# Splitting the second halves of short products around the score matmuls, and taking the projection before the first maxima

## The chip, the cores and the metric

The kernel runs on one core of a Trainium2 chip. The metric is device time in microseconds (us) of one execution, from launch to the last output in memory. TensorE (PE in the rows; PEld is its weight load), VectorE (DVE), ScalarE (ACT), GpSimd (POOL) and SyncE (SP, which issues the transfers) each run their own instruction stream and meet through semaphores.

## The reference

One transformer block on x of shape (8, 512, 256), fp32: a layer norm, then multi-head attention and a gated feed-forward layer side by side, and a residual.

```python
xn  = layernorm(x)                               # over the 256 channels
qkv = xn @ qkv_w + qkv_b                         # 16 heads of 16 channels
att = softmax(q @ k.T / 4) @ v                   # per head, 512 x 512 scores
out = x + (att @ proj_w + proj_b) \
        + (silu(xn @ (w_gate/127).T) * (xn @ (w_up/127).T)) @ (w_down/127).T
```

The feed-forward hidden size is 768; its weights are integers from -127 to 127.

## The kernel before, in words

**Precision by parts.** An fp32 operand is kept as a high and a low fp32r part, and a product is a sum of terms high x high, low x high and high x low. A weight that is exact in its high part needs two terms instead of three; the feed-forward weights are, and the kernel finds that out at run time and takes the shorter branch.

**Rows and steps.** "Row" is one of the 8 batch entries. The work of a row is cut into 16 steps of a software pipeline (`STEPS`), in which a step s works on four heads (group s // 4) and 128 keys (s % 4). In each step TensorE does, in this order (`step`, L1326 on):

1. `scores_t(s, 0)`: the transposed scores of two heads, two matmuls into `st_bank` (L1077). It waits until ScalarE has taken the previous content (`exp_done`).
2. the second half of the step's product (`end_product`, L1264)
3. `scores(.., 0)`: scores for six steps later, two matmuls into `s_bank` (L1094), needed for the row maxima alone. It waits until VectorE has reduced the previous content (`max_done`).
4. `probs_v`: probabilities times values of the step before, eight matmuls into `o_bank` in the trace (L1110)
5. in four of the steps a small transpose of maxima (L1208)
6. `scores_t(s, 1)`, then `scores(.., 1)`, as 1 and 3, for the other two heads
7. the first half of the next step's product (`begin_product`, L1254)

For long products (down, and q1 with k1) item 2 comes after item 3 instead.

ScalarE takes the exponential of each transposed score bank (L743), one instruction per item 1 or 6, and VectorE takes the maxima of each score bank (L889), again two per step. There is one `st_bank` and one `s_bank`, so each score matmul waits for the reader of the last one.

**Products in halves.** A product is made with matmuls of 64 rows of contraction, two at a time in the upper and lower half of the array, each writing its own PSUM bank. The first half pass (`half_product(spec, 0)`) sends rows 0 to 63 to bank A and 64 to 127 to bank B; the second (`swap=1`) exchanges them. As both passes add to the same banks, the second starts with a wait for `half_made`, which the last matmul of the first increments. A "term" below is one such pair of matmuls.

**The table.** `STEADY` (L65) says in which step each product ("chunk") stands: up4 with gate4 in step 0, v1 in 1, up5 in 2, the transposes of xn in 3, proj0 (of the row before) in 4, q0 in 5, k0 in 6, proj1 in 7, q1 with k1 in 8, down0 and down1 in 9 and 10, up0 to up3 with their gates in 11 to 14, v0 in 15. A half pass has 6 terms of 2 x 256 columns for v, q0, k0 and proj; 4 terms of 2 x 512 columns for up with gate. The last entry of a chunk is its PSUM banks of `dense`, three in all: proj0 uses (0, 1) and q0 behind it (1, 2); proj1 uses (0, 1), and q1 with k1 behind it 2 and 0.

**Who takes a product.** ScalarE takes v, q, k and up in slot 0 of their step, after the exponential of item 1; the gate goes to ScalarE and VectorE after item 6. proj and down are added to `resid` by VectorE (L919), in slot 0 after the maxima of item 3: in `step` of VectorE `maxima(row, s, slot // 2)` comes first, and then `take(row, chunk)` for `("proj", "down")`.

## Time and profile before

| | |
|---|---|
| median of 3 runs | 610.33 us (609.66 to 615.7) |
| profiled execution, its own time | 611.8 us |
| its span | 610.0 us |
| TensorE busy | 579.2 us (95%), 5012 matmuls |
| VectorE busy | 427.1 us (70%) |
| ScalarE busy | 421.2 us (69%) |
| GpSimd busy | 300.1 us (49%) |
| mean granted TensorE clock | 0.991 of full speed |
| chain that ended last | TensorE 82%, ScalarE 6%, VectorE 5% |

The page of the profile gives these sums; the rest is read from the timeline, which lists instructions by start time and merges equal ones that follow each other. A matmul's printed duration is longer than the distance to the next one, since they are pipelined, so what a block of matmuls costs on TensorE is the distance from its start to the start of the next block. A row of the timeline that starts later than the one before it would allow has its idle time in brackets only if no matmul is still in flight.

### The profile page before, as it was taken

The page shows a single profiled execution, that of the slowest core. Times are in us where ns is not written, and L with a number is a line of the kernel's source. Part 1 is how long each engine was busy: PE and PEld are TensorE (multiplying, and loading weights), DVE is VectorE, ACT ScalarE, POOL GpSimd, SP SyncE. Part 2 cuts the span into 40 slices and gives each one's busy share as a digit, 9 for nine tenths or more (in the row PEclk, how much of TensorE's full clock was granted, in tenths as well). Part 3 has the DMA queues.
Part 4 walks back from the last instruction along what each step waited for, and adds up shares of the span by engine and source line. Part 5 has one row for each costly group of instructions (what it writes and reads, how often), then busy time and mean ns, then how long its engine had stood idle before and what let it go on. Part 6 is the DMA issues. An engine that isn't in the chain of part 4 may idle for free.

```text
span 610.0 us, 14095 instructions
## 1 busy us (share of the span) xinstructions
PE 579.2 (95%) x5012; PEld 344.2 (56%) x5012; DVE 427.1 (70%) x514; ACT 421.2 (69%) x604; POOL 300.1 (49%) x303
## 2 busy tenths in 40 slices
PE   7888799999999999999999999999999999998896
PEld 6655356555755557555665567555665557553533
DVE  5886667777777767777777776777677866777722
ACT  3556675887577866878667866787658875776562
POOL 3234737644475526754465535844376444354210
PEclk9999999999999999999999999999999999999989
DMA  8790146122822147222742128221661118220101
GB/s 263 240 153 2 37 139 172 32 52 81 230 84 54 53 134 161 53 52 76 190 133 53 35 108 204 52 53 53 183 157 31 29 70 233 66 54 19 54 2 37
DMA packets 38609, 59.20 MB, mean 97 GB/s; under 512 B 6320, under 2 KB 21680, under 8 KB 38576
## 3 DMA queue, kind: packets, MB, share of 16 engines
q1 hardware_dynamic: 38576, 58.75, 36.0%
q8 instruction: 22, 0.36, 0.3%
q14 instruction: 11, 0.09, 0.1%
HBM read 37.23 MB, written 20.97 MB: 95 GB/s over the span
## 4 chain that ended last, share of the span: by engine, by line
PE 82%; ACT 6%; DVE 5%; issue 3%; DMA 1%; POOL 1%; SPq 0%; DVEq 0%; POOLq 0%
PE dense L1136 33%; PE o_bank L1110 19%; PE st_bank L1077 14%; PE s_bank L1094 10%; ACT probs L743 3%; PE dense L1120 2%; DVE resid L919 1%; DVE neg_max L889 1%; PE dense L1200 1%; DMA probs<-in_L_attn_qkv_w 1%; PE dense L1208 1%; POOL xn L637 1%; ACT max_whole L784 1%; ACT probs L821 1%; PE dense L1189 0%
## 5 line engine op out<-in xcount | busy, mean ns | idle before, releaser
L889 DVE TENSOR_REDUCE neg_max<-s_bank 128x2 f32<-128x1024 f32 x250 | 306.0, 1224 | 135.7 <-PE s_bank L1094 135.7
L743 ACT ACTIVATE probs<-st_bank 128x1024 f32<-128x1024 f32 x250 | 256.8, 1027 | 120.0 <-PE st_bank L1077 117.3
L1110 PE MATMUL o_bank<-probs,v_ones 128*32 128x512 f32 x1024 | 138.1, 612 | 0.0
L1077 PE MATMUL st_bank<-q_stack,k_stack 50*128 50x512 f32 x500 | 121.1, 480 | 8.3 <-ACT probs L743 7.0
L1077 PEld LDWEIGHTS st_bank<-q_stack,k_stack 50*128 50x128 f32 x500 | 47.4, 184 | 115.0 <-ACT probs L743 72.8
L1094 PE MATMUL s_bank<-k_stack,q_stack 48*128 48x512 f32 x500 | 109.1, 431 | 1.9 <-DVE neg_max L889 1.8
L652 POOL TENSOR_TENSOR hid_tl<-gated,hid_th 128x512 fp32r<-128x512 f32 x48 | 61.7, 1286 | 35.1 <-ACT hid_th L835 35.1
L646 POOL TENSOR_TENSOR gated<-gated,hid 128x512 f32<-128x512 f32 x48 | 61.7, 1285 | 34.6 <-DVE gated L911 18.5
L1094 PEld LDWEIGHTS s_bank<-k_stack,q_stack 48*128 48x128 f32 x500 | 47.3, 184 | 25.5 <-DVE neg_max L889 20.1
L1136 PE MATMUL dense<-xn_th,w_uh 64*128 64x512 f32 x176 | 57.0, 403 | 1.2 <-ACT v_ones L775 0.8
L1136 PE MATMUL dense<-xn_th,w_gh 64*128 64x512 f32 x176 | 57.3, 405 | 0.0
L1136 PE MATMUL dense<-xn_tl,w_gh 64*128 64x512 f32 x176 | 54.9, 391 | 0.0
L1136 PE MATMUL dense<-xn_tl,w_uh 64*128 64x512 f32 x176 | 54.9, 391 | 0.0
L664 POOL TENSOR_TENSOR qk_parts<-raw_d,qk_parts 128x512 fp32r<-128x512 f32 x28 | 35.8, 1289 | 27.8 <-ACT qk_parts L812 27.8
L679 POOL TENSOR_TENSOR o_norm<-o_blocks,inv_sum 128x256 f32<-128x256 f32 x31 | 19.3, 623 | 59.0 <-DVE inv_sum L934 58.7
L705 POOL TENSOR_TENSOR resid<-resid,p_bias 128x256 f32<-128x256 f32 x32 | 22.9, 737 | 48.3 <-DMA resid<-in_L_attn_x 48.3
L1110 PEld LDWEIGHTS o_bank<-probs,v_ones 128*32 128x32 f32 x1024 | 20.2, 108 | 37.1 <-issue 26.8
L637 POOL TENSOR_SCALAR xn<-xn,moments,rstd 128x256 f32<-128x256 f32 x28 | 33.9, 1224 | 1.3 <-POOL rstd L631 1.3
L911 DVE SCALAR_TENSOR_TENSOR gated<-gated,dense 128x512 f32<-128x512 f32 x48 | 32.2, 670 | 3.4 <-ACT gated L789 2.1
L1136 PEld LDWEIGHTS dense<-xn_tl,w_gh 64*128 64x128 f32 x176 | 32.4, 184 | 3.7
L1136 PEld LDWEIGHTS dense<-xn_tl,w_uh 64*128 64x128 f32 x176 | 32.4, 184 | 3.3
L930 DVE STREAM_TRANSPOSE o_blocks<-o_bank 128x512 f32<-128x512 f32 x31 | 22.0, 709 | 16.1 <-PE o_bank L1110 16.1
(147 smaller groups left out, 855.9 us busy)
## 6 DMA issues: line engine op xcount, KB each, us to landing
q_spread<-qk_parts SPq DMA_DIRECT2D x16, 512.0 KB, 3.5
k_spread<-qk_parts SPq DMA_DIRECT2D x16, 512.0 KB, 3.7
q_stack<-q_spread SPq DMA_DIRECT2D x64, 128.0 KB, 3.1
k_stack<-k_spread SPq DMA_DIRECT2D x64, 128.0 KB, 3.3
q_stack<-q_spread SPq DMA_DIRECT2D x64, 64.0 KB, 3.3
k_stack<-k_spread SPq DMA_DIRECT2D x64, 64.0 KB, 3.3
resid<-in_L_attn_x SPq DMA_DIRECT2D x16, 256.0 KB, 3.6
out<-resid SPq DMA_DIRECT2D x15, 256.0 KB, 2.2
```

The source lines that it names most:

```text
L637: nc.gpsimd.tensor_scalar(xn[:, t, :], xn[:, t, :], moments[:, t, 0:1], rstd[:, t:t + 1], ALU.subtract, ALU.mult).then_inc(xn_done, 1)
L646: nc.gpsimd.tensor_tensor(gated[:, m % 2, :], gated[:, m % 2, :], hid[:, m % 2, :], ALU.mult).then_inc(hid_product, 1)
L652: nc.gpsimd.tensor_tensor(hid_t[1][:, m, :], gated[:, m % 2, :], hid_t[0][:, m, :].bitcast(F32), ALU.subtract).then_inc(hid_low, 1)
L664: nc.gpsimd.tensor_tensor(low, whole[:, WHOLE_AT[kind, i], :], high.bitcast(F32), ALU.subtract).then_inc(split_low, 1)
L705: nc.gpsimd.tensor_tensor(resid[:, t, :], resid[:, t, :], p_bias[:, :], ALU.add).then_inc(resid_ready, 1)
L743: nc.scalar.activation(probs[:, s % 2, 2 * half:2 * half + 2, :], transposed_bank(row, s, half)[:, :, :], ACT.Exp, scale=SCALE).then_inc(e ...
L889: nc.vector.tensor_reduce(neg_max[:, g % 2, :, NT * pair + qt], score_bank(row, half)[:, :, :], AX_X, ALU.max, negate=True).then_inc(max_d ...
L911: nc.vector.scalar_tensor_tensor(part, part, 1.0, bank, ALU.add, ALU.mult).then_inc(dve_free, 1)
L1077: done = nc.tensor.matmul(transposed_bank(row, s, half)[:, r, :], k_stack[rows, pair, P * kt:P * (kt + 1)], q_stack[rows, pair, :], start= ...
L1094: done = nc.tensor.matmul(score_bank(row, half)[:, r, :], q_stack[rows, pair, P * qt:P * (qt + 1)], k_stack[rows, pair, :], start=True, st ...
L1110: done = nc.tensor.matmul(o_bank[32 * j:32 * (j + 1), :], v_ones[:, kt, 8 * (g // 2) + 2 * j + g % 2, :], probs[:, (s - 1) % 2, j, :], sta ...
L1136: done = nc.tensor.matmul(banks[h], stationary(h, a, k)[rows], moving(h, b, k)[rows], start=swap == 0 and n == 0, stop=swap == 1 and n == ...
```

## The change

A table `ENDS` gives for each short kind of product how many terms of the second half pass stand ahead of `scores_t(s, 0)` and how many behind `scores(.., 0)`; what is left stays between them. (4, 2) for v, q, k: four terms, the transposed scores, the scores, two terms. (6, 0) for proj: all six terms, the transposed scores, the scores. (0, 1) for up: the transposed scores, three terms, the scores, one term. Long products stay as they were. The wait for `half_made` stands before the first term of the pass, wherever that is. On VectorE the take of proj moves ahead of the maxima of its slot; the take of down stays behind.

```diff
--- before.py
+++ after.py
@@ -80,6 +80,9 @@
     (14, 0, "up", 3, 1, (1,)), (14, 0, "gate", 3, 1, (0,)), (14, 1, "max", 0, 1, (2,)),
     (15, 0, "v", 0, 1, (1, 2)),
 ]
+
+
+ENDS = {"v": (4, 2), "q": (4, 2), "k": (4, 2), "proj": (6, 0), "up": (0, 1)}
 
 TOGETHER = {("up", i): ("gate", i) for i in range(KH)} | {("q", 1): ("k", 1)}
 WPREP = ("wgate", "wup", "wdown")
@@ -1027,10 +1030,13 @@
                         averaged = averaged_at(row, s, slot)
                         if averaged is not None:
                             statistics_done(averaged)
+                        for chunk in chunks_at(row, s, slot):
+                            if chunk[2] == "proj":
+                                take(row, chunk)
                         if slot in (0, 2) and pair_ahead(row, s, slot // 2):
                             maxima(row, s, slot // 2)
                         for chunk in chunks_at(row, s, slot):
-                            if chunk[2] in ("proj", "down"):
+                            if chunk[2] == "down":
                                 take(row, chunk)
                         if measured and measured[0] == 0:
                             dve.wait_ge(x_in, 16 * measured[1])
@@ -1121,13 +1127,16 @@
                                                 stop=n == len(parts) - 1 and k == tiles - 1)
                 return done
 
-            def half_product(spec, swap):
+            def terms_in(spec):
+                return sum(len(those) for _, those in spec[3])
+
+            def half_product(spec, swap, some=slice(None)):
 
 
 
                 banks, stationary, moving, stages = spec
                 terms = [(ready if n == 0 else None, term) for ready, those in stages for n, term in enumerate(those)]
-                for n, (ready, (a, b, k)) in enumerate(terms):
+                for n, (ready, (a, b, k)) in list(enumerate(terms))[some]:
                     if ready is not None and swap == 0:
                         pe.wait_ge(*ready)
                     for r in range(2):
@@ -1261,10 +1270,20 @@
                     pe.wait_ge(ot_low1, row.at)
                 half_product(spec_of(row, chunk, exact), 0).then_inc(half_made, 1)
 
-            def end_product(row, chunk, exact):
-
-                pe.wait_ge(half_made, products_up_to(row, chunk))
-                half_product(spec_of(row, chunk, exact), 1).then_inc(dense_done, len(made_together(row, chunk)))
+            def end_product(row, chunk, exact, part):
+
+
+                spec = spec_of(row, chunk, exact)
+                of_all = terms_in(spec)
+                ahead, behind = (0, of_all) if long_product(chunk) else ENDS[chunk[2]]
+                some = (slice(0, ahead), slice(ahead, of_all - behind), slice(of_all - behind, of_all))[part]
+                if some.start == some.stop:
+                    return
+                if some.start == 0:
+                    pe.wait_ge(half_made, products_up_to(row, chunk))
+                done = half_product(spec, 1, some)
+                if some.stop == of_all:
+                    done.then_inc(dense_done, len(made_together(row, chunk)))
 
             def project_first_half():
 
@@ -1329,14 +1348,16 @@
                     here = product_at(row, s)
                     if here and s == 0:
                         begin_product(row, here, exact)
+                    if here:
+                        end_product(row, here, exact, 0)
                     if row.has(0):
                         scores_t(row, s, 0)
-                    if here and not long_product(here):
-                        end_product(row, here, exact)
+                    if here:
+                        end_product(row, here, exact, 1)
                     if pair_ahead(row, s, 0):
                         scores(row, s, 0)
-                    if here and long_product(here):
-                        end_product(row, here, exact)
+                    if here:
+                        end_product(row, here, exact, 2)
                     if after_scores(row, s):
                         scores_t(row, s, 1)
                     if row.like == ROWS and s == 0:
```

In the three pairs of fences below a name such as `dense<-xn_th,w_gh` is the bank written and the operands read; L1136 before and L1145 now is the matmul of `half_product`, L1077 and L1083 the transposed scores (`st_bank`), L1094 and L1100 the scores (`s_bank`), L1110 and L1116 the probabilities times values (`o_bank`).

TensorE, a q product (also v and k), from the first half pass to `probs_v`, before:

```order
L1136 MATMUL dense<-w_qkvh,xn_th 128x256 x4
L1136 MATMUL dense<-w_qkvh,xn_tl 128x256 x4
L1136 MATMUL dense<-w_qkvl,xn_th 128x256 x4
L1077 MATMUL st_bank<-q_stack,k_stack 128x512 x2
L1136 MATMUL dense<-w_qkvh,xn_th 128x256 x4
L1136 MATMUL dense<-w_qkvh,xn_tl 128x256 x4
L1136 MATMUL dense<-w_qkvl,xn_th 128x256 x4
L1094 MATMUL s_bank<-k_stack,q_stack 128x512 x2
L1110 MATMUL o_bank<-probs,v_ones 32x512 x4
```

and now:

```order
L1145 MATMUL dense<-w_qkvh,xn_th 128x256 x4
L1145 MATMUL dense<-w_qkvh,xn_tl 128x256 x4
L1145 MATMUL dense<-w_qkvl,xn_th 128x256 x4
L1145 MATMUL dense<-w_qkvh,xn_th 128x256 x4
L1145 MATMUL dense<-w_qkvh,xn_tl 128x256 x4
L1083 MATMUL st_bank<-q_stack,k_stack 128x512 x2
L1100 MATMUL s_bank<-k_stack,q_stack 128x512 x2
L1145 MATMUL dense<-w_qkvl,xn_th 128x256 x4
L1116 MATMUL o_bank<-probs,v_ones 32x512 x4
```

Nothing stands between the two half passes any more; the transposed scores have moved back by four terms, and two terms have moved behind the scores.

TensorE, the second half pass of an up product with its gate, before:

```order
L1077 MATMUL st_bank<-q_stack,k_stack 128x512 x2
L1136 MATMUL dense<-xn_th,w_gh 128x512
L1136 MATMUL dense<-xn_th,w_uh 128x512
L1136 MATMUL dense<-xn_th,w_gh 128x512
L1136 MATMUL dense<-xn_th,w_uh 128x512
L1136 MATMUL dense<-xn_tl,w_gh 128x512
L1136 MATMUL dense<-xn_tl,w_uh 128x512
L1136 MATMUL dense<-xn_tl,w_gh 128x512
L1136 MATMUL dense<-xn_tl,w_uh 128x512
L1094 MATMUL s_bank<-k_stack,q_stack 128x512 x2
```

and now:

```order
L1083 MATMUL st_bank<-q_stack,k_stack 128x512 x2
L1145 MATMUL dense<-xn_th,w_gh 128x512
L1145 MATMUL dense<-xn_th,w_uh 128x512
L1145 MATMUL dense<-xn_th,w_gh 128x512
L1145 MATMUL dense<-xn_th,w_uh 128x512
L1145 MATMUL dense<-xn_tl,w_gh 128x512
L1145 MATMUL dense<-xn_tl,w_uh 128x512
L1100 MATMUL s_bank<-k_stack,q_stack 128x512 x2
L1145 MATMUL dense<-xn_tl,w_gh 128x512
L1145 MATMUL dense<-xn_tl,w_uh 128x512
```

The scores have moved one term forward.

VectorE around the take of proj0 (`resid<-dense,resid`), before:

```order
L889 TENSOR_REDUCE neg_max<-s_bank 128x2
L898 ISA
L917 ISA
L919 TENSOR_TENSOR resid<-dense,resid 128x512
L926 REGISTER_ALU
L929 REGISTER_ALU
L930 STREAM_TRANSPOSE o_blocks<-o_bank 128x512
L888 REGISTER_ALU
L889 TENSOR_REDUCE neg_max<-s_bank 128x2
```

and now:

```order
L901 ISA
L920 ISA
L922 TENSOR_TENSOR resid<-dense,resid 128x512
L891 ISA
L892 TENSOR_REDUCE neg_max<-s_bank 128x2
L929 REGISTER_ALU
L932 REGISTER_ALU
L933 STREAM_TRANSPOSE o_blocks<-o_bank 128x512
L891 REGISTER_ALU
L892 TENSOR_REDUCE neg_max<-s_bank 128x2
```

The maxima of the step's first scores now stand behind the take, and so behind the end of the whole projection product.

## Rows read from the trace of the kernel before

**Rows 1.** Timeline of TensorE, step 5 into 6 (k0): start us, us, engine, line, instruction.
```profile
283.61 1.06 PE L1110 MATMUL o_bank<-probs,v_ones 128*32 128x512 f32 x8
284.61 0.50 PE L1077 MATMUL st_bank<-q_stack,k_stack 50*128 50x512 f32 x2
285.00 0.50 PE L1094 MATMUL s_bank<-k_stack,q_stack 48*128 48x512 f32 x2
285.35 0.40 PE L1136 MATMUL dense<-xn_th,w_qkvh 64*128 64x256 f32 x4
...
286.22 0.50 PE L1077 MATMUL st_bank<-q_stack,k_stack 50*128 50x512 f32 x2
286.56 0.40 PE L1136 MATMUL dense<-xn_th,w_qkvh 64*128 64x256 f32 x4
...
287.26 0.39 PE L1094 MATMUL s_bank<-k_stack,q_stack 48*128 48x512 f32 x2
287.58 1.07 PE L1110 MATMUL o_bank<-probs,v_ones 128*32 128x512 f32 x8
```

**Rows 2.** Timeline of ScalarE in step 5: the exponential of the second transposed scores.
```profile
285.14 1.03 ACT L743 ACTIVATE probs<-st_bank 128x1024 f32<-128x1024 f32 x1 [0.85 <-PE st_bank L1077]
```

**Rows 3.** Timeline of TensorE, step 13 into 14 (up3), one row earlier.
```profile
251.16 0.51 PE L1077 MATMUL st_bank<-q_stack,k_stack 50*128 50x512 f32 x2
251.55 0.50 PE L1094 MATMUL s_bank<-k_stack,q_stack 48*128 48x512 f32 x2
251.89 0.39 PE L1136 MATMUL dense<-xn_th,w_uh 64*128 64x512 f32 x1
...
252.82 0.46 PE L1077 MATMUL st_bank<-q_stack,k_stack 50*128 50x512 f32 x2
253.12 0.43 PE L1136 MATMUL dense<-xn_th,w_uh 64*128 64x512 f32 x1
...
254.09 0.40 PE L1094 MATMUL s_bank<-k_stack,q_stack 48*128 48x512 f32 x2
```

**Rows 4.** Timeline of VectorE: the maxima just before the scores at 251.55.
```profile
250.27 1.23 DVE L889 TENSOR_REDUCE neg_max<-s_bank 128x2 f32<-128x1024 f32 x1 [0.49 <-PE s_bank L1094]
```

**Rows 5.** Timeline of TensorE over proj0 and the start of q0.
```profile
276.96 0.70 PE L1136 MATMUL dense<-w_ph,ot_parts 64*128 64x256 f32 x8
...
278.92 0.40 PE L1094 MATMUL s_bank<-k_stack,q_stack 48*128 48x512 f32 x2
...
280.66 0.48 PE L1094 MATMUL s_bank<-k_stack,q_stack 48*128 48x512 f32 x2
281.43 0.51 PE L1136 MATMUL dense<-xn_th,w_qkvh 64*128 64x256 f32 x4 [0.29 <-DVE resid L919]
```

**Rows 6.** Timeline of VectorE beside it.
```profile
279.36 1.23 DVE L889 TENSOR_REDUCE neg_max<-s_bank 128x2 f32<-128x1024 f32 x1 [0.97 <-PE s_bank L1094]
280.50 0.68 DVE L919 TENSOR_TENSOR resid<-dense,resid 128x512 f32<-128x512 f32 x1
```

**Rows 7.** Timeline of TensorE: proj1 starts its first half, and q1 behind it.
```profile
289.36 0.64 PE L1136 MATMUL dense<-w_ph,ot_parts 64*128 64x256 f32 x8
...
293.77 0.72 PE L1136 MATMUL dense<-xn_th,w_qkvh 64*128 64x512 f32 x4
```

**Rows 8.** Timeline of TensorE around a wait for half_made (step 5, q0).
```profile
282.01 0.41 PE L1136 MATMUL dense<-xn_tl,w_qkvh 64*128 64x256 f32 x4
...
282.49 0.49 PE L1136 MATMUL dense<-xn_th,w_qkvh 64*128 64x256 f32 x4
282.81 0.40 PE L1136 MATMUL dense<-xn_th,w_qkvl 64*128 64x256 f32 x4
```

**Rows 9.** Timeline of the weight loads (PEld) at the same place.
```profile
282.47 0.30 PEld L1136 LDWEIGHTS dense<-xn_th,w_qkvh 64*128 64x128 f32 x4 [0.15 <-PE dense L1136]
```

**Rows 10.** Timeline of TensorE in step 9, a long product, where no score matmul waits.
```profile
300.22 0.40 PE L1077 MATMUL st_bank<-q_stack,k_stack 50*128 50x512 f32 x2
300.46 0.40 PE L1094 MATMUL s_bank<-k_stack,q_stack 48*128 48x512 f32 x2
```

## The prediction

> **What bounds the kernel now.** The table of busy times comes first: TensorE is busy for 95% of the span and holds 82% of the chain that ended last, ScalarE and VectorE are busy for about 70%. So a step lasts as long as TensorE's stream of blocks, and the question is which distances between blocks are longer than the work in them. That is read from the timeline, start to start.
>
> Take the step around k0 [rows 1]. A pair of score matmuls costs 0.24 us where nothing waits [rows 10]. After `probs_v` (1.00 us, 283.61 to 284.61) the second transposed scores take 0.39 and the second scores 0.35; the first half pass takes 0.87 (285.35 to 286.22), although the second, of the same matmuls, takes 0.70 (286.56 to 287.26); the first transposed scores take 0.34 and the first scores 0.32. The 0.17 us in the first half pass is a stall: the exponential of the bank filled at 284.61 runs from 285.14 to 286.17 [rows 2], and only then, at 286.22, may the bank be written. So **transposed scores must be at least 1.61 us apart**. Each score matmul that really waits costs 0.10 us more than 0.24 as well, since its weight load no longer lies under earlier matmuls. In the same way **scores must be about 1.71 us apart**: 0.44 from their start to VectorE (278.92 to 279.36 in [rows 5, 6]), 1.23 for the maxima, 0.05 back (251.50 to 251.55 in [rows 3, 4]).
>
> The first half pass of an up product is longer (0.93) and meets the 1.61 nearly by itself [rows 3]: the second transposed scores at 251.16, the first at 252.82. There the second scores are late, at 0.39 behind the transposed ones instead of 0.34, and take 0.34 instead of 0.24, because VectorE ends at 251.50 [rows 4].
>
> **The change part by part.** In every sum below a pair of scores is 0.24 without a wait and 0.34 with one or directly behind `probs_v`; the last block ahead of `probs_v` pays 0.09 more (0.32 instead of 0.24 at 287.26 to 287.58 [rows 1]), whichever block that is.
>
> *The wait for half_made.* In v, q, k and proj it now follows directly on the first half pass. How long TensorE then stands is not in the trace, but its parts are. The last pair of the first half starts near 282.13 (the row at 282.01 holds two pairs, 0.12 apart [rows 8]) and its record ends at 282.42. The load that waited for it starts at 282.47 [rows 9], so 0.34 after the last pair started, where the next pair would have started after 0.12: 0.22 lost. The first four matmuls behind that wait take 0.32 to the next block instead of 0.24 [rows 8], so 0.08 to 0.10 more. I take **0.32 us per wait**, with 0.10 (the load alone) and 0.45 as ends, the upper one if the semaphore takes 0.13 longer to come back when the engine is empty. There are six such products in a row of the batch: 1.9 us, which is what the moves must earn back.
>
> What the trace shows of this tail is the end of a record and a semaphore. The Trainium skill (TensorE: Matmul & The Clock Gate, Single matmul latency and Back-to-back issue gap) gives an isolated matmul of 256 columns (398 + 256) / 2.4 = 272 ns against a gap of 109 ns in a stream. By that page alone the exposed tail would be an estimated 0.16 us instead of 0.32, and the sum 6 x 0.16 x 7 = 7 us lower; the rows here show 0.28 for the record, and the semaphore and the load besides.
>
> *v, q and k (4, 2).* The new step is 0.34 (transposed) + 0.24 (scores: the last ones are now 0.24 + 0.32 + 1.00 + 0.34 = 1.90 back, over 1.71) + 0.70 + 0.32 + 0.47 (four terms) + 0.24 + 0.24 (the other bank was filled 2.07 before, over 1.61) + 0.32 (two terms) + 1.00 = 3.87, against 3.97 now (283.61 to 287.58 [rows 1]). The gap to the next transposed scores is 0.24 + 0.24 + 0.32 + 1.00 = 1.80, again over 1.61. That is 0.10; with the unrounded 0.235 for a pair it is 0.12. I take **0.12 for each of k0, v1 and v0: 0.36**. The takes on ScalarE have cover: an exponential (from 0.5 after the matmul, 1.03 long) and a take (by VectorE's of the same size 0.6) end 2.1 after the transposed scores, and the next exponential can start 2.3 after.
>
> *proj (6, 0) and its take.* For proj0 [rows 5, 6]: the first half starts at 276.96 and lasts 0.70, the wait 0.32, the second half 0.70, so the transposed scores stand at 278.68 and the scores at 278.92, which is where they are today. The product is complete at about 278.84, VectorE takes it from 278.88, and 0.60 later (0.68 less the 0.09 by which the next instruction overlaps, as 279.36 + 1.23 = 280.59 is followed at 280.50) starts the maxima: 279.48 instead of 279.36. They end at 280.71; the second scores start at 280.76 instead of 280.66. This is the new wait, 0.10 us. But q0 today starts at 281.43 only, because it writes a bank of proj0 that VectorE empties behind the maxima; now that bank is long free and q0 starts at 280.76 + 0.34 = 281.10: **0.33 gained**. q0 itself pays its 0.32 and loses the penalty of 0.10 twice: its stretch to `probs_v` goes from 2.18 (281.43 to 283.61) to 0.70 + 0.32 + 0.47 + 0.24 + 0.24 + 0.32 = 2.29: 0.11 lost. Together **0.22**.
>
> For proj1 [rows 7]: 289.36 + 0.70 + 0.32 + 0.70 = 291.08 for the transposed scores, take from 291.28, maxima from 291.88 to 293.11, second scores 293.16, and q1 with k1 at 293.50 instead of 293.77: **0.27**.
>
> *up (0, 1).* One term goes behind the scores, so the scores are 0.24 + 0.32 + 1.00 + 0.34 = 1.90 ahead of the next and the wait of [rows 4] goes. What is late next is the exponential: 0.34 + 0.24 + 0.93 = 1.51 is under 1.61, so the transposed scores wait for it. From transposed scores to the next ones past `probs_v`: 1.61 + 0.34 + 0.70 + 0.24 + 0.32 + 1.00 = 4.21, against 2.93 + 0.33 + 1.00 = 4.26 now [rows 3]. **0.05 for each of six: 0.3.** So two thirds of what is moved here is given back at once.
>
> *Long products and the xn step* keep their order: 0. SyncE and GpSimd get nothing new; a proj take that comes sooner lets its store be issued sooner, beside other work.
>
> The sum is 0.36 + 0.22 + 0.27 + 0.3 = 1.15 us per row of the batch. v0, q, k and up0 to up3 occur in rows 0 to 6, proj in rows 1 to 7, v1, up4 and up5 in all eight: seven sets, 8.05 us. From the profiled execution's 611.8 that gives 603.8; the median of the runs was 1.5 below that execution, so **602.3 us**.
>
> **The rivals.**
>
> *A. The predicted chain of small gains, 599 to 605.* For it: every distance used stands in a row, and the step with no waiting scores shows that satisfied waits cost nothing [rows 10].
>
> *B. Nothing measurable, 605 to 610.* The drain costs its upper end, 0.45: 6 x 0.13 x 7 = 5.5 us less gain, leaving 2.5 (607.8). Or ScalarE's takes fall behind in the up steps, where the product is complete 0.24 later. For it: the drain with nothing behind it is the only length not seen whole. Against it: the load at 282.47 started within 0.06 of the record's end.
>
> *C. Slower, 612 to 625.* The weight loads behind the half_made wait and around the split groups are no longer pulled under earlier matmuls: each score pair in the changed place, and each term group behind it, pays 0.10 although its wait is satisfied. That is four more in v and k steps (3.87 + 0.40 = 4.27 against 3.97, three times 0.3), two more in up steps (4.41 against 4.26, six times 0.15), four in q0 and two in each proj (0.8, against the 0.49 of the pairs): 0.9 + 0.9 + 0.3 = 2.1 us per row, 15 us, so 625 at worst. It decides from about 11 such loads per row, where the 1.15 is gone. Against it stands [rows 10]; for it only that satisfied waits straight behind an emptied engine are not in the trace.
>
> *D. More than predicted, 595 to 599.* The drain costs only its lower end, 0.10, because the load may pass earlier than in [rows 9]: 6 x 0.22 x 7 = 9 us more at the most (593). Against it: the second pass cannot start before the first has ended.
>
> **How the numbers follow.** Chances: A 0.55, B 0.24, C 0.09, D 0.12. The likeliest case gives 602.3. The range reaches from 597.5, into D, to 608.5, into B, and leaves out C, the top of B and the bottom of D, about 0.2. What a measurement of this kernel can tell from no change is 1%, 6.1 us: faster means under 604.2, slower over 616.4. A's upper edge lies just past that line, so of A some 0.47 counts as faster, with D 0.59, and 0.01 of B; same is the rest of A and B and a part of C, 0.32; slower 0.08.
>
> **What would show it.** In the profile of the changed kernel: in the k0 step the distance from the end block of the first half pass to the second should be 0.32 longer than the matmuls in them, the transposed scores and the scores there should stand 0.24 apart, and `probs_v` to `probs_v` should be 3.87. q0's first matmul should follow the second scores by 0.34 with no idle time released by `resid`. In up steps scores should follow the second transposed ones at once and the first transposed ones should wait for ScalarE. Wrong would be the sum if score pairs without a wait took 0.34, if the take of proj delayed the second scores by over 0.3, or if the gap in front of the second half pass were over 0.45.

## The result, and the profile after

The changed kernel takes 606.27 us against 611.95 for the one before (medians of 13 runs each); the ratio is 0.9904, 95% interval 0.9878 to 0.993. The ratio leaves out one run of the changed kernel, 611.86, which fell into the chip's slower state. A second set of runs gave 0.992 (0.989 to 0.9951). The prediction was 602.3, from 597.5 to 608.5, and 8 us gained; by the two ratios 5.9 and 4.9 us were.

The profiled execution has a span of 603.0 us, 7.0 less than before. Not all of it is the change: the first half of the first up4, ahead of which no edited instruction stands, starts at 47.74 instead of 49.65. The first `probs_v` starts at 54.17 instead of 56.05, so the two edited steps between gain nothing (6.43 against 6.40). In the traces of this case that second point lies anywhere between 53.7 and 56.3, whatever the kernel. From there to the end 5.1 us are gone.

The chain that ended last, from the page of the changed kernel, by engine:

```profile
PE 84%; DVE 6%; ACT 3%; issue 2%; DMA 1%; POOL 1%; SPq 0%; DVEq 0%; POOLq 0%
```

ScalarE's share has halved, from 6% to 3%: the exponential was what the transposed scores waited for. VectorE's has gone from 5% to 6%.

The best instrument here is the step table. Each entry is the distance in us from one `probs_v` to the next on TensorE, the median of rows 1 to 4 of the batch. An entry is named by the product whose halves lie in it, so it also holds the second transposed scores and second scores of the step before. Such medians agree within some 0.02 between runs of one kernel, while whole runs of one kernel scatter over 1%. The granted clock was 1.00 in these rows in every trace used here.

| | before | changed | difference | predicted |
|---|---|---|---|---|
| k0, v1 | 3.99, 3.99 | 3.88, 3.88 | -0.22 | -0.24 |
| v0 | 4.20 | 4.20 | 0 | -0.12 |
| proj0 + q0 | 4.11 + 4.34 | 4.17 + 4.32 | +0.05 | -0.22 |
| proj1 + q1k1 | 4.20 + 5.45 | 4.09 + 5.30 | -0.26 | -0.27 |
| up0, up1, up2, up3, up5 | 21.49 | 21.37 | -0.12 | -0.25 |
| up4 | 4.61 | 4.35 | -0.26 | -0.05 |
| xn, down0, down1 | 13.63 | 13.65 | +0.02 | 0 |
| row of the batch | 69.99 | 69.20 | -0.80 | -1.15 |

**k0** came as worked out. TensorE in the changed kernel, the stretch that answers to [rows 1]:

```profile
279.42 1.06 PE L1116 MATMUL o_bank<-probs,v_ones 128*32 128x512 f32 x8
280.42 0.50 PE L1083 MATMUL st_bank<-q_stack,k_stack 50*128 50x512 f32 x2
280.76 0.39 PE L1100 MATMUL s_bank<-k_stack,q_stack 48*128 48x512 f32 x2
280.99 0.40 PE L1145 MATMUL dense<-xn_th,w_qkvh 64*128 64x256 f32 x4
...
281.46 0.40 PE L1145 MATMUL dense<-xn_tl,w_qkvh 64*128 64x256 f32 x4
281.92 0.50 PE L1145 MATMUL dense<-xn_th,w_qkvh 64*128 64x256 f32 x4
...
282.49 0.40 PE L1083 MATMUL st_bank<-q_stack,k_stack 50*128 50x512 f32 x2
282.73 0.40 PE L1100 MATMUL s_bank<-k_stack,q_stack 48*128 48x512 f32 x2
282.97 0.40 PE L1145 MATMUL dense<-xn_tl,w_qkvh 64*128 64x256 f32 x4
283.30 0.64 PE L1116 MATMUL o_bank<-probs,v_ones 128*32 128x512 f32 x4
```

Read start to start: transposed scores 0.34, scores 0.23 (0.35 before, when they waited for VectorE), then ten terms and the wait for `half_made` in 1.50 (280.99 to 282.49), which without the wait would be 1.17. So **the wait costs 0.33**; 0.32 was taken. It shows as 281.46 to 281.92, 0.46 where four matmuls take 0.23, and as 0.34 instead of 0.23 for the four behind it. The transposed scores and the scores stand 0.24 apart, neither waiting.

**up** came as worked out in kind. The stretch that answers to [rows 3]:

```profile
247.40 0.51 PE L1083 MATMUL st_bank<-q_stack,k_stack 50*128 50x512 f32 x2
247.74 0.40 PE L1100 MATMUL s_bank<-k_stack,q_stack 48*128 48x512 f32 x2
247.97 0.39 PE L1145 MATMUL dense<-xn_th,w_gh 64*128 64x512 f32 x1
...
249.02 0.50 PE L1083 MATMUL st_bank<-q_stack,k_stack 50*128 50x512 f32 x2
249.36 0.39 PE L1145 MATMUL dense<-xn_th,w_gh 64*128 64x512 f32 x1
```

The second scores follow after 0.34 and take 0.23, where they took 0.34 before. But the first transposed scores stand at 247.40 + 1.62: the exponential's distance, now binding in full. The step takes 4.21, as forecast, but up0 and up1 gain 0.01 and nothing.

**proj0 and q0** did not. TensorE in the changed kernel, the stretch that answers to [rows 5]:

```profile
272.74 0.70 PE L1145 MATMUL dense<-w_ph,ot_parts 64*128 64x256 f32 x8
...
273.73 0.74 PE L1145 MATMUL dense<-w_ph,ot_parts 64*128 64x256 f32 x8
274.30 0.40 PE L1145 MATMUL dense<-w_pl,ot_parts 64*128 64x256 f32 x4
274.54 0.40 PE L1083 MATMUL st_bank<-q_stack,k_stack 50*128 50x512 f32 x2
274.77 0.40 PE L1100 MATMUL s_bank<-k_stack,q_stack 48*128 48x512 f32 x2
...
276.11 0.50 PE L1083 MATMUL st_bank<-q_stack,k_stack 50*128 50x512 f32 x2
276.72 0.49 PE L1100 MATMUL s_bank<-k_stack,q_stack 48*128 48x512 f32 x2
277.06 0.45 PE L1145 MATMUL dense<-xn_th,w_qkvh 64*128 64x256 f32 x4
```

and VectorE beside it, as in [rows 6]:

```profile
274.85 0.69 DVE L922 TENSOR_TENSOR resid<-dense,resid 128x512 f32<-128x512 f32 x1 [0.68 <-PE dense L1145]
275.45 1.22 DVE L892 TENSOR_REDUCE neg_max<-s_bank 128x2 f32<-128x1024 f32 x1
```

The idle time at q0 that `resid` ended is gone, as foretold. From the start of the first half pass to q0 it is now 4.32 instead of 4.47 in [rows 5], though: 0.15 gained and not 0.33. Two places are late. The two passes took 1.80 (272.74 to 274.54), where 1.72 was reckoned and 1.74 is what proj1 takes; no run here shows what the 0.06 more than at proj1 are. And the last matmul's record ends at 274.70, the take starts at 274.85: 0.15 for a step that costs VectorE 0.04 to 0.05 at the scores. It starts the maxima 0.60 later, and they end at 276.67, just before the second scores at 276.72. From the first matmul of the product those scores stand at 3.98, against 3.70 before and 3.80 forecast. q0 itself, from its first matmul to `probs_v`, takes 2.36 (277.06 to 279.42) instead of 2.18, where 2.29 was forecast.

### The profile page after: what moved, and what is told of

It is laid out like the page before. It is cut to its first block, busy times and chain, and to the rows that moved or that the text cites. A ratio compares the mean times of both kernels' runs of the same rounds, so it can differ in the third digit from the quotient of the medians.

```text
span 603.0 us, 14095 instructions
## 1 busy us (share of the span) xinstructions
PE 574.4 (95%) x5012; PEld 346.2 (57%) x5012; DVE 430.5 (71%) x514; ACT 423.4 (70%) x604; POOL 300.2 (50%) x303
## 4 chain that ended last, share of the span: by engine, by line
PE 84%; DVE 6%; ACT 3%; issue 2%; DMA 1%; POOL 1%; SPq 0%; DVEq 0%; POOLq 0%
PE dense L1145 37%; PE o_bank L1116 19%; PE st_bank L1083 14%; PE s_bank L1100 10%; DVE neg_max L892 4%; PE dense L1126 2%; PE dense L1209 1%; PE dense L1217 1%; DMA probs<-in_L_attn_qkv_w 1%; ACT probs L746 1%; POOL xn L640 1%; ACT probs L824 1%; PE dense L1198 0%; DVE w_gl L925 0%; DMA q_stack<-max_tl 0%
## 5 line engine op out<-in xcount | busy, mean ns | idle before, releaser
L1116 PE MATMUL o_bank<-probs,v_ones 128*32 128x512 f32 x1024 | 137.6, 610 | 0.0
L1083 PE MATMUL st_bank<-q_stack,k_stack 50*128 50x512 f32 x500 | 118.9, 471 | 6.3 <-ACT probs L746 5.4
L1083 PEld LDWEIGHTS st_bank<-q_stack,k_stack 50*128 50x128 f32 x500 | 47.3, 184 | 110.7 <-ACT probs L746 67.9
L1100 PE MATMUL s_bank<-k_stack,q_stack 48*128 48x512 f32 x500 | 104.3, 412 | 2.5 <-DVE neg_max L892 1.1
L1145 PE MATMUL dense<-xn_tl,w_gh 64*128 64x512 f32 x176 | 61.8, 391 | 0.0
L1145 PE MATMUL dense<-xn_tl,w_uh 64*128 64x512 f32 x176 | 61.8, 391 | 0.0
L1100 PEld LDWEIGHTS s_bank<-k_stack,q_stack 48*128 48x128 f32 x500 | 47.5, 185 | 17.6 <-DVE neg_max L892 12.6
L1145 PE MATMUL dense<-xn_th,w_uh 64*128 64x512 f32 x176 | 55.8, 396 | 0.8 <-ACT v_ones L778 0.8
L1145 PE MATMUL dense<-xn_th,w_gh 64*128 64x512 f32 x176 | 56.0, 397 | 0.0
L1116 PEld LDWEIGHTS o_bank<-probs,v_ones 128*32 128x32 f32 x1024 | 20.2, 108 | 34.8 <-issue 21.1
L1145 PEld LDWEIGHTS dense<-xn_tl,w_gh 64*128 64x128 f32 x176 | 32.5, 185 | 3.9
L1145 PEld LDWEIGHTS dense<-xn_tl,w_uh 64*128 64x128 f32 x176 | 32.5, 185 | 3.0
```

Source lines behind the costliest of these rows:

```text
L1083: done = nc.tensor.matmul(transposed_bank(row, s, half)[:, r, :], k_stack[rows, pair, P * kt:P * (kt + 1)], q_stack[rows, pair, :], start= ...
L1100: done = nc.tensor.matmul(score_bank(row, half)[:, r, :], q_stack[rows, pair, P * qt:P * (qt + 1)], k_stack[rows, pair, :], start=True, st ...
L1116: done = nc.tensor.matmul(o_bank[32 * j:32 * (j + 1), :], v_ones[:, kt, 8 * (g // 2) + 2 * j + g % 2, :], probs[:, (s - 1) % 2, j, :], sta ...
L1145: done = nc.tensor.matmul(banks[h], stationary(h, a, k)[rows], moving(h, b, k)[rows], start=swap == 0 and n == 0, stop=swap == 1 and n == ...
```

## Experiments

All step figures are the medians of rows 1 to 4, as in the table. The kernels of experiments 1 to 8 ran once each, so their whole times are not compared.

**1. The up products alone.** `ENDS` with (0, 1) for up and (0, 0) for the rest, the take as before.

```diff
-ENDS = {"v": (4, 2), "q": (4, 2), "k": (4, 2), "proj": (6, 0), "up": (0, 1)}
+ENDS = {"v": (0, 0), "q": (0, 0), "k": (0, 0), "proj": (0, 0), "up": (0, 1)}
```

> Only the up products are split, (0, 1); v, q, k, proj and the take as before. Theory 1 (the parts are independent, and each step's gain belongs to its own edit): up steps 12 to 14 and 2 last 4.21 us as in the changed kernel (4.25 before), with the exponential as their new limit; step 0 keeps the changed kernel's 4.35 (4.60 before); k0 stays at 3.99, proj0 with q0 at 8.45, proj1 with q1 at 9.65. A row of the batch then lasts 69.6 us instead of 70.0. Theory 2 (the parts lean on each other): step 0 gains only because v0 ahead of it was changed too, and stays at 4.6; a row 69.85.

Measured: a row 69.91. up2 4.21 and up3 4.23 as expected, but up4 4.60, not 4.35. up1 (4.29) and up5 (4.25) gain nothing either, where 4.21 was expected. So the parts do lean on each other, and the large gain at up4 is not of the up edit. The 0.03 that up5 gains in the changed kernel isn't either: it comes back in experiment 2 (4.22), with v1 split and up not. This kernel and the changed one at the start of up4's step, second transposed scores, second scores and the first matmul of up4; first this kernel:

```profile
260.16 0.50 PE L1080 MATMUL st_bank<-q_stack,k_stack 50*128 50x512 f32 x2
260.56 0.49 PE L1097 MATMUL s_bank<-k_stack,q_stack 48*128 48x512 f32 x2
261.15 0.49 PE L1142 MATMUL dense<-xn_th,w_uh 64*128 64x512 f32 x1
```

then the changed kernel:

```profile
255.80 0.50 PE L1083 MATMUL st_bank<-q_stack,k_stack 50*128 50x512 f32 x2
256.14 0.39 PE L1100 MATMUL s_bank<-k_stack,q_stack 48*128 48x512 f32 x2
256.54 0.49 PE L1145 MATMUL dense<-xn_th,w_uh 64*128 64x512 f32 x1
```

Here the loop over the batch branches back, between the second scores and up4. With v0 unsplit the scores wait for VectorE (0.40 behind the transposed ones), and up4 is 0.59 behind them. With v0's two terms behind the first scores they do not wait (0.34), and up4 follows after 0.40. That the instructions around the branch can be worked off ahead only when the scores do not block the stream fits this, since the 0.19 between 0.59 and 0.40 is more than the 0.10 of an exposed load; in the trace of before, where the written-out rows at the end of the batch have no branch between, up4 follows after 0.34 (469.97 to 470.31) with the scores waiting just the same. No run here shows the branch by itself.

**2. v, q and k alone.**

```diff
-ENDS = {"v": (4, 2), "q": (4, 2), "k": (4, 2), "proj": (6, 0), "up": (0, 1)}
+ENDS = {"v": (4, 2), "q": (4, 2), "k": (4, 2), "proj": (0, 0), "up": (0, 0)}
```

> Only v, q0 and k0 are split, (4, 2); up, proj and the take as before. Theory 1: k0 and v1 last 3.88 (3.99 before), v0 4.20 as before, since its first half waits 0.10 for a bank and that wait used to lie under the exponential's. q0 loses about 0.1 to the drain but still starts late behind the take of proj0: proj0 with q0 8.55 (8.45 before). A row: 70.0 - 0.22 + 0.1 = 69.9. Theory 2 (the drain costs more where the engine is not kept waiting anyway): v0 slower than 4.25 and k0 over 3.92.

Measured: a row 69.85, k0 3.88, v0 4.20. up4 is 4.35, which settles experiment 1: v0's split gives up4 its 0.25. It is the two terms behind the scores and not the four ahead, since up4 keeps its 4.35 in experiment 7, where none stand ahead. v1 is 4.03 and not 3.88: its second scores wait again, as up4's last term no longer stands behind the first ones. And q0 is 4.56, 0.23 slower than before, twice the expected loss.

v0 gains nothing in its own step because another wait stands there. A weight load of the changed kernel:

```profile
252.39 0.30 PEld L1145 LDWEIGHTS dense<-w_qkvh,xn_th 64*128 64x128 f32 x4 [0.28 <-ACT max_whole L787]
```

v0's first half writes the bank from which ScalarE has just copied the maxima. Its ten terms and the wait for `half_made` take 1.61 instead of k0's 1.50. Before, the load waited for the same copy, and the 0.11 lay under the wait for the exponential; with that gone it counts. In the trace of before:

```profile
256.20 0.30 PEld L1136 LDWEIGHTS dense<-w_qkvh,xn_th 64*128 64x128 f32 x4 [0.21 <-ACT max_whole L784]
```

**3. proj alone**, (6, 0), with its take ahead.

```diff
-ENDS = {"v": (4, 2), "q": (4, 2), "k": (4, 2), "proj": (6, 0), "up": (0, 1)}
+ENDS = {"v": (0, 0), "q": (0, 0), "k": (0, 0), "proj": (6, 0), "up": (0, 0)}
```

> Only proj, (6, 0), with its take ahead of the maxima; v, q, k and up as before. Theory 1: proj1 with q1 lasts 9.39 as in the changed kernel (9.65 before). proj0 with q0: the changed kernel's 8.49 less what q0's drain costs there, 0.19: 8.30 (8.45 before). A row 70.0 - 0.26 - 0.15 = 69.6. Theory 2 (the loss at proj0 is in the take and not in q0's drain): 8.45 or more.

Measured: a row 69.59, half of the whole change's gain from this part alone. The three parts by themselves gain 0.08, 0.14 and 0.40, together 0.62 of the whole change's 0.80; nearly all the rest is v1, which gains its 0.11 only with up4's last term behind the scores. proj1 with q1k1 9.40, proj0 with q0 4.18 + 4.07 = 8.25. So **the loss is in q0's split**: 4.07 unsplit, 4.32 split. TensorE at q0 in this kernel:

```profile
280.83 0.51 PE L1083 MATMUL st_bank<-q_stack,k_stack 50*128 50x512 f32 x2
281.45 0.50 PE L1100 MATMUL s_bank<-k_stack,q_stack 48*128 48x512 f32 x2
281.80 0.44 PE L1145 MATMUL dense<-xn_th,w_qkvh 64*128 64x256 f32 x4
...
282.54 0.41 PE L1083 MATMUL st_bank<-q_stack,k_stack 50*128 50x512 f32 x2
282.79 0.48 PE L1145 MATMUL dense<-xn_th,w_qkvh 64*128 64x256 f32 x4
...
283.57 0.41 PE L1100 MATMUL s_bank<-k_stack,q_stack 48*128 48x512 f32 x2
```

The second scores are 0.62 behind the transposed ones, since the maxima are late behind the take. By the time the first half pass is through, the transposed scores are already 1.71 apart (280.83 to 282.54), over the 1.61 that the exponential asks for. They wait for nothing, and they cover the empty part of the way of `half_made`: what is left of it is 0.09 for the load (282.79 to 283.11 is 0.32 instead of 0.23). There is nothing to be had by going ahead of them.

**4. The take of proj behind the maxima again**, all splits kept.

```diff
-                            if chunk[2] == "proj":
-                                take(row, chunk)
...
-                            if chunk[2] == "down":
+                            if chunk[2] in ("proj", "down"):
```

> The changed kernel with the take of proj behind the maxima of its slot, as it was before; all splits kept. Theory 1 (the take sets when the next product may start, as the prediction had it): the second scores start 0.27 earlier (no take ahead of the maxima), but q0 and q1 wait for the take again: maxima end at 1.90 after the transposed scores, the take 0.6 later, q0 0.1 after that, at 2.6, against 2.52 in the changed kernel: proj0 with q0 8.57 (8.49), proj1 with q1 9.47 (9.39). Theory 2 (the move of the take buys nothing): both the same within 0.03 or shorter.

Measured: proj0 with q0 8.74 (8.49 in the changed kernel), proj1 with q1k1 9.54 (9.39), a row 69.66: the move of the take is worth 0.46 a row, and without it the whole change would have gained 0.34. The expectation had the direction and not the size: 0.25 and 0.15 lost against 0.08 each. TensorE:

```profile
279.61 0.49 PE L1097 MATMUL s_bank<-k_stack,q_stack 48*128 48x512 f32 x2
280.37 0.50 PE L1142 MATMUL dense<-xn_th,w_qkvh 64*128 64x256 f32 x4 [0.27 <-DVE resid L922]
```

and VectorE:

```profile
279.47 0.68 DVE L922 TENSOR_TENSOR resid<-dense,resid 128x512 f32<-128x512 f32 x1
```

The second scores no longer wait for late maxima, and q0 waits for the take instead, as before the change.

**5. The order of two waits at the take.** In the loop's rows a semaphore's value is worked out in registers. The take of proj waited for the product first and for the old residual second, so the arithmetic for the second came after the first wait was over. The residual's wait, long satisfied, now comes first.

```diff
+                if kind == "proj":
+                    dve.wait_ge(dve_free, count(of_row(row, -1), freed_by_dve, kind="down", index=i))
                 if first_on_act(row.like, kind):
                     dve.wait_ge(act_done, count(row, first_on_act, chunk))
...
-                    else:
-                        dve.wait_ge(dve_free, count(of_row(row, -1), freed_by_dve, kind="down", index=i))
```

> The changed kernel, but VectorE waits for the old residual (long done) before it waits for the projection, so that the arithmetic on registers for both waits is over when the product comes. Theory 1 (the missing 0.1 us at the take is that arithmetic, which stands behind the wait for the product in the loop's rows): the take starts 0.05 instead of 0.15 after the last matmul's record, the second scores behind the transposed ones come 0.1 sooner, proj0 with q0 lasts 8.40 (8.49), proj1 with q1 9.29 (9.39), a row 69.0 (69.20). Theory 2 (the delay is the matmul's real end, later than its modelled record): no step moves by more than 0.02.

Measured: proj0 with q0 8.40, proj1 with q1k1 9.30, a row 69.04. The last matmuls of the projection in this kernel:

```profile
277.00 0.41 PE L1144 MATMUL dense<-w_pl,ot_parts 64*128 64x256 f32 x4
```

and the take:

```profile
277.44 0.69 DVE L921 TENSOR_TENSOR resid<-dense,resid 128x512 f32<-128x512 f32 x1 [0.57 <-PE dense L1144]
```

The record ends at 277.41 and the take starts 0.03 later, where it was 0.15. The missing 0.1 was arithmetic standing behind a wait. The trace of the changed kernel has it as a record of VectorE's sequencer, on the line of the second wait. It starts 0.05 after the matmul's record has ended (274.70), and the take 0.05 after its end:

```profile
L920 DVEq FUSED_REGOPS  x1: 53/53/53, 274.7 to 274.7; - x1
```

In the rows written out at the end of the batch, where the values are constants, it is the other way round. There the take follows the matmul's record after 0.04 in the changed kernel and after 0.11 in this one, at each of the four takes. So the edit gains 0.1 in the loop's rows and gives back 0.07 in the others.

**6. q0 with (0, 2)**: the second half behind the transposed scores again, two terms behind the scores.

```diff
-ENDS = {"v": (4, 2), "q": (4, 2), "k": (4, 2), "proj": (6, 0), "up": (0, 1)}
+ENDS = {"v": (4, 2), "q": (4, 2), "k": (4, 2), "proj": (6, 0), "up": (0, 1), ("q", 0): (0, 2)}
...
-                ahead, behind = (0, of_all) if long_product(chunk) else ENDS[chunk[2]]
+                ahead, behind = (0, of_all) if long_product(chunk) else ENDS.get(chunk[2:4], ENDS.get(chunk[2]))
```

> The changed kernel with (0, 2) instead of (4, 2) for q0 alone: its second half starts behind the transposed scores, four terms stand between them and the scores, two behind. Theory 1 (going ahead pays only where the transposed scores would wait for the exponential, and behind proj0 they do not, since the second scores are late there already, so that the drain is a bare loss): q0 4.09 (4.32), k0 stays at 3.88 since the two terms behind the scores relieve it, a row 68.97. Theory 2 (q0 is late for another reason): q0 over 4.25.

Measured: q0 4.11, k0 3.86, a row 69.03.

**7. v, q and k with (0, 2).**

```diff
-ENDS = {"v": (4, 2), "q": (4, 2), "k": (4, 2), "proj": (6, 0), "up": (0, 1)}
+ENDS = {"v": (0, 2), "q": (0, 2), "k": (0, 2), "proj": (6, 0), "up": (0, 1)}
```

> The changed kernel with (0, 2) for v, q and k alike. Theory 1 (ahead trades the exponential's wait for the drain, which are nearly equal): k0 and v1 last 1.00 + 1.61 + 0.34 + 0.47 + 0.24 + 0.32 = 3.98 (3.88 with four terms ahead), v0 4.19 (4.20), q0 4.09 (4.32). So a row gets 0.2 for the two that are worse and loses 0.24 for q0: 69.2 as before. Theory 2 (the gain of k0 and v1 is in the two terms behind the scores alone): they stay at 3.88.

Measured: k0 3.98, v1 3.99, v0 4.20, q0 4.11, a row 69.25. The two terms behind the scores alone thus buy k0 and v1 nothing (3.99 before): the exponential takes it all back. TensorE, k0's transposed scores:

```profile
212.41 0.50 PE L1083 MATMUL st_bank<-q_stack,k_stack 50*128 50x512 f32 x2
...
214.03 0.49 PE L1083 MATMUL st_bank<-q_stack,k_stack 50*128 50x512 f32 x2 [0.18 <-ACT probs L746]
```

1.62 apart, by the exponential. From the second transposed scores through the second scores, the first half pass and the first transposed scores it takes 1.62 + 0.34 = 1.96 here. With four terms ahead the same blocks and the wait for `half_made` take 0.34 + 0.23 + 0.70 + 0.33 + 0.24 = 1.84. The two waits are nearly the same size, and going ahead wins 0.1, no more.

**8. Is the wait for half_made empty time?** Two more matmuls between the passes of k0, into a bank that nobody reads.

```diff
+                if part == 0 and chunk[2:4] == ("k", 0):
+                    for _ in range(2):
+                        nc.tensor.matmul(dense[:, 2, 0:TOK // 2], w_qkv[0][0:HALF, 0, 0:P],
+                                         xn_t[0][0:HALF, 0, 0:TOK // 2], start=True, stop=True, tile_position=(0, 0))
```

> The changed kernel with two more matmuls of 64 rows and 256 columns between the two half passes of k0, ahead of its wait for half_made; they write a PSUM bank that nobody reads. Theory 1 (TensorE stands there for 0.22 us until the first half has drained and its semaphore is back): the two, 0.117 us each, fit into it; k0 lasts 3.88 to 3.92. Theory 2 (the 0.33 us are a cost of loads or of order and not an empty wait): k0 lasts 3.88 + 0.23 = 4.11.

Measured: k0 3.86, with two matmuls more than the 3.88 of the changed kernel. TensorE (L1284 are the two):

```profile
213.82 0.40 PE L1145 MATMUL dense<-xn_tl,w_qkvh 64*128 64x256 f32 x4
214.06 0.40 PE L1284 MATMUL dense<-xn_th,w_qkvh 64*128 64x256 f32 x2
214.29 0.50 PE L1145 MATMUL dense<-xn_th,w_qkvh 64*128 64x256 f32 x4
214.62 0.40 PE L1145 MATMUL dense<-xn_th,w_qkvl 64*128 64x256 f32 x4
```

The two fill 0.23 us, and the second pass starts 0.47 after 213.82, as it did without them (281.46 to 281.92). So 0.23 of the 0.33 is an empty engine, and 0.10 (214.29 to 214.62 is 0.33 instead of 0.23) is the load that could not be pulled ahead of the wait.

**9. The changed kernel again, with both repairs, and with work in the gap.** Three kernels on one chip. The second has the edits of 5 and 6. The third moves besides the transpose of the third group's maxima into the gap of proj1:

```diff
-    (6, 0, "k", 0, 1, (0, 1)), (6, 1, "max", 2, 0, (2,)),
+    (6, 0, "k", 0, 1, (0, 1)), (6, 2, "max", 2, 0, (2,)),
```

> The changed kernel as it is, on the same chip as the next two. Both theories: 0.990 of before, as measured, a row of the batch 69.2 us.

> The changed kernel with the two repairs together: VectorE's wait for the projection last, and (0, 2) for q0. Theory 1 (they act at different places: one shortens the second scores' wait behind both takes, the other takes q0's drain away): q0 4.11 less up to 0.10, where the shorter wait may bring the exponential's back (the transposed scores are then 0.52 + 0.34 + 0.75 = 1.61 apart, just at the limit), so 4.01 to 4.05; proj1 with q1 9.30; a row 68.88; 7 rows x 0.32 = 2.2 us less than the changed kernel, 0.9865 of before. Theory 2 (with both, the exponential's wait returns in full): q0 4.11, a row 68.95, 0.9875.

> The kernel with both repairs, and the small transpose of the third group's maxima moved from behind probs_v of step 6 into the gap between the two half passes of proj1; ScalarE's and GpSimd's parts of it move one slot later. Theory 1 (the gap is empty time): 0.21 leaves the stretch behind probs_v, and in the gap it costs what goes over 0.22: the transpose and the change to 128 rows and back, 0.21 + 0.09 + 0.09, so 0.17; proj1 4.09 - 0.21 + 0.17 = 4.05. Theory 2 (a change of tile inside the gap drains the engine anyway, so the transpose starts in the drained engine and the gap is paid twice): proj1 4.2 or more. A row 68.85 or 69.0; 0.986 or 0.988 of before.

| | median, us | ratio to before | interval | a row | proj0 + q0 | proj1 |
|---|---|---|---|---|---|---|
| changed | 606.51 | 0.992 | 0.989 to 0.9951 | 69.24 | 8.50 | 4.09 |
| both repairs | 603.5 | 0.9868 | 0.9829 to 0.9906 | 68.88 | 8.19 | 4.10 |
| and the gap used | 604.03 | 0.9887 | 0.9846 to 0.9928 | 68.68 | 8.19 | 3.95 |

Both repairs give 0.36 a row over the changed kernel, and all six of its runs (602.85 to 604.4) lie below all twelve of that one (604.55 to 611.56). q0 is 4.01, so the two add up, although the transposed scores now just meet the exponential again. The third gains 0.15 more at proj1, not the expected 0.04. TensorE there (L1216 is the transpose):

```profile
216.12 0.64 PE L1144 MATMUL dense<-w_ph,ot_parts 64*128 64x256 f32 x8
216.60 0.40 PE L1144 MATMUL dense<-w_pl,ot_parts 64*128 64x256 f32 x4
216.93 0.28 PE L1216 MATMUL dense<-ident,neg_max 128*16 128x128 f32 x1
217.14 0.74 PE L1144 MATMUL dense<-w_ph,ot_parts 64*128 64x256 f32 x8
...
217.95 0.40 PE L1082 MATMUL st_bank<-q_stack,k_stack 50*128 50x512 f32 x2
```

From 216.12 to 217.95 it is 1.83, against 1.74 in the changed kernel without the transpose: in the gap the transpose costs 0.09 where it cost 0.21. The two changes of tile, which the expectation had added at 0.18, are within that 0.09; the remaining 0.03 is spread over the blocks around. By the step table the third kernel is the fastest, by 0.20 a row. But the median of rows 1 to 4 does not see a single long step. In row 6 of this trace up1 takes 5.64 instead of 4.30, since its transposed scores wait for the transfer of the fourth group's maxima:

```profile
517.02 0.50 PE L1082 MATMUL st_bank<-q_stack,k_stack 50*128 50x512 f32 x2 [1.37 <-DMA q_stack<-max_tl]
```

That eats what the six rows had gained, and no other trace here has it at that step. Whether moving the transpose made it likelier is not shown. The whole-run ratios do not tell the third kernel from the second: their intervals overlap, and its median is the higher one.

## Why the prediction was right, and where its terms were off

**The frame held.** Distances of 1.61 for transposed scores and 1.71 for scores, 0.24 for a pair without a wait, 0.10 for an exposed load: all came back in the changed trace. Only the 1.61 is not a floor for every pair: where the first one has no exposed load, the next stands 1.57 behind it (274.54 to 276.11). The time lies in the range, and the direction was right. The gain was 4.9 to 5.9 us instead of 8, which is right in kind and by a third to two thirds too large. Of the 4.0 us between 602.3 and 606.27, 2.4 are gain that did not come. The other 1.6 are the kernel before, which stood at 610.33 by 3 runs and at 611.95 by 13.

**The wait for half_made (0.32).** Measured 0.33, and by experiment 8 made up as it was put: 0.23 empty, 0.10 for the load. The estimate by the Trainium skill (TensorE: Matmul & The Clock Gate, Single matmul latency and Back-to-back issue gap), 0.16 for the tail, leaves out the semaphore and the load; the traces decide for 0.33.

**k0 and v1 (0.12 each).** Measured 0.11. Right.

**v0 (0.12).** Measured 0. The step that failed is "I take 0.12 for each of k0, v1 and v0": the row of k0 was carried over to v0, whose first half waits 0.11 for ScalarE's copy of the maxima. In the trace of before that wait was hidden under a longer one.

**proj0 and q0 (0.22).** Measured a loss of 0.05. Both terms failed. "0.33 gained" was 0.15: the latency of the take was taken from the scores (0.04) and was 0.15, by experiment 5 register arithmetic behind the wait, and the two passes took 0.08 longer than reckoned. "0.11 lost" was 0.18. What the split costs q0 is more, 0.25 by experiment 3. The prediction had compared q0 split with q0 as it was before, without asking whether q0 still had a wait to escape once its neighbour had changed; unsplit it would have been 4.07.

**proj1 (0.27).** Measured 0.26. That is luck, a hit with two misses in it that cancel: the take was 0.1 late here as well, so that from the first matmul of proj1 to q1k1 0.15 were gained (4.26 instead of 4.41) and not 0.27, and q1k1 started its half pass without the exposed load it had before (1.39 instead of 1.50).

**up (0.05 each, 0.3).** 0.02 on average for five of them. "What is late next is the exponential" was right and took nearly all of it. The row of up3 was carried over to steps that are not like it, as k0's was to v0. up1 has 1.71 between its transposed scores, 1.72 in the trace of before, and gains 0. Its scores open a new group of heads and have two waits, one of them for the transfer of the maxima. The exponential ends at 240.47, and the weight load of the changed kernel starts 0.11 behind that instead of 0.05:

```profile
240.58 0.22 PEld L1083 LDWEIGHTS st_bank<-q_stack,k_stack 50*128 50x128 f32 x2 [0.45 <-issue]
```

A second wait handled behind the late one is what experiment 5 found on VectorE; that it is the same here is not shown by a run of its own. up4's 0.26 was not foreseen at all, and belongs to v0.

**The rivals.** The measured time lies in the span of B (605 to 610), just outside A's (599 to 605). By the prediction's own line, faster under 604.2, it counts as same, to which it gave 0.32. But B's causes, a dearer drain or late takes on ScalarE, are not what happened; the missing 0.35 us a row are v0, q0 and the up steps, less what up4 gave. C, loads exposed everywhere, is refuted by the 0.24 between satisfied score pairs in k0. D is refuted by 0.33.

## What to carry to other kernels

- In a stream that several engines meet, a wait that is removed hands its place to the next: write down every distance that must hold (here 1.61 and 1.71), and work each step out for the neighbours as they will be, not as they are in the old trace. A wait that shows nothing may lie under another.
- When an engine waits for its own last result, the wait is worth filling: here 0.23 us of small matmuls were free.
- Put the semaphore that comes last at the end of several waits, when their values are computed in registers; with constant values the order that was better here was the opposite one.

## What the runs showed of the hardware

- Waiting for its own matmuls costs TensorE 0.33 us behind a 256-column matmul: 0.23 in which it can do other work, 0.10 for the weight load that does not pass the wait.
- Putting 0.21 us of transpose in 128 rows and its two changes of tile into such a gap cost 0.09 in all.
- Two waits against register values on VectorE, the later event first, start the instruction 0.13 to 0.15 us after the matmul's record; the other way round 0.04. With constant values it was 0.04 and 0.11.
- A step's median repeats within about 0.02 us, while whole runs scatter by a little over 1%. Small edits to a long loop are better judged by step distances than by whole runs, if the single long steps are looked at as well.
